# Routing an expert layer by a list of tokens: one-hot matmuls and gathers in place of a scatter of rows

## The chip, the cores and the metric

The kernel runs on one core of a Trainium2 chip. Its engines are TensorE (PE, with its weight loads as PEld), VectorE (DVE), ScalarE (ACT), GpSimd (POOL) and SyncE (SP). The metric is the time of one execution on the device in microseconds, lower is better.

## The reference

A decoder block over 32 sequences of 128 tokens with 128 features, 4096 tokens in all. Each of three layers is followed by a residual add and a layer norm.

```python
x = _layernorm(x + attn(x, Wq, Wk, Wv, Wo, betas))     # 16 heads, segments of 64
x = _layernorm(x + xattn(x, ctx, ctx, Wq, Wk, Wv))     # retention with decay
x = _layernorm(x + ffn(x, Wg, bg, W1, b1, W2, b2))

# ffn: top-1 routing over 8 experts, hidden size 512
gate_scores = softmax(x @ Wg + bg)
top1_idx = argmax(gate_scores)
top1_mask = one_hot(top1_idx, 8)
top1_weight = sum(gate_scores * top1_mask)
h = silu(einsum('btd,edh->bteh', x, W1) + b1)
o = einsum('bteh,ehd->bted', h, W2) + b2
y = sum(o * top1_mask[..., None], axis=2) * top1_weight
```

## The kernel before

The kernel is five phases, one after the other: `attention_phase`, `retention_phase`, `gate_phase`, `expert_phase` and `finish_phase`. Each opens a block in which every engine has a program of its own; engines wait for each other by semaphores, and a phase begins when all engines have ended the one before. Sequences lie as tiles of 128 tokens (partitions) by 128 features; groups are of four tiles (`G`).

`retention_phase` works over eight groups. PE transposes the context and x1, projects, scores, and multiplies; VectorE first computes the norm (`norm_dve`, lines 137 to 156) and then stages x1 (line 1007) and scales. GpSimd, before its own loop, fills a tile `padding` with zeros and a row number (lines 880 and 882). SyncE loads the expert weights after the last context tile (line 872) and then writes `padding` to the DRAM tensor `sorted_x` (line 874).

`gate_phase` norms again, keeps x2 in `x2_row` with the token's row in a 129th column, and computes logits. VectorE then runs one chain from line 1181 to 1247: softmax, the one-hot row of the best expert (`hot`), a prefix over the 32 batches in five doubling steps, and the row in expert order of each token (`place`); PE ranks tokens inside a batch by two matmuls (lines 1109 and 1110). The experts' tokens are padded to whole tiles of 128, at most `NT` = 39 tiles. GpSimd scatters the 32 tiles of `x2_row` into `sorted_x`, one indirect transfer each (line 1142).

`expert_phase` has 39 steps. SyncE loads `xs` from `sorted_x` in four pieces. For each tile ACT stages x and the biases (lines 1367 and 1374), PE transposes (1327), VectorE stages the expert's W1 (1410) and the transposed x (1414), PE computes the hidden layer (1343), ACT applies Silu (1392), PE multiplies by W2 (1353), and VectorE adds the bias (1433). GpSimd casts the row numbers and scatters the tile into `y_rows` (lines 1309 to 1314). `finish_phase` reads `y_rows` back, adds, norms and stores.

The order of work inside an engine is the order of its program; nothing is reordered. The steps of a loop are written once and unrolled in pairs by `run_steps`.

Of the kernel before, what the change touches and what calls it, by code (L numbers as in the profile page):

```python
# [6 lines left out]
F32 = mybir.dt.float32  # L7
F32R = mybir.dt.float32r
U32 = mybir.dt.uint32
# [23 lines left out]
NT = B + E - 1  # L33


def shape_constants():
# [25 lines left out]
    below = (tok[:, None] < tok[None, :]).astype(np.float32)  # L62
    ones = np.ones((P, P), np.float32)
    upto = row(np.arange(E)[None, :] <= np.arange(E)[:, None])
    tile_at = row(np.arange(NT))
    full = row(P * np.arange(B))
    token_row = tok[:, None] + P * np.arange(B)[None, :]
    spare_row = P * B + tok[:, None] + P * np.arange(NT)[None, :]
    cols = [ident, z_sum] + tabs + [decay, iota, below, ones, upto, tile_at, full, token_row, spare_row]
# [5 lines left out]
for _n, _w in (("ident", P), ("z_sum", SEG * H), ("qcos", P), ("qsin", P), ("kcos", P), ("ksin", P),  # L75
               ("decay", P), ("iota", E), ("below", P), ("ones", P), ("upto", E * E),
               ("tile_at", NT), ("full", B), ("token_row", B), ("spare_row", NT)):
    CONST_AT[_n] = (_at, _at + _w)
    _at += _w
# [732 lines left out]
def retention_phase(nc, const, r_all, stats, ctx_in, Wq, Wk, Wv, preload, sorted_x):  # L812
# [3 lines left out]
    with ExitStack() as ctx:  # L816
# [23 lines left out]
        padding = sb("padding", [P, NT, D + 1])  # L840
# [4 lines left out]
        padded, preloaded = sem("padded"), sem("preloaded")  # L845
# [12 lines left out]
        def _(sp):  # L858
# [172 lines left out]
def gate_phase(nc, const, r_all, x2_row, stats, top, tile_expert, biases, Wg, bg, b1, sorted_x):  # L1031
# [6 lines left out]
    with ExitStack() as ctx:  # L1038
# [14 lines left out]
        total, inv, index = (sb(n, [P, B]) for n in ("total", "inv", "index"))  # L1053
        b1_rows = sb("b1_rows", [E * FT, P])
        count, upto_batch = sb("count", [P, B, E]), [sb(f"upto_batch{i}", [P, B, E]) for i in range(2)]
        is_full, tiles, by_expert = sb("is_full", [P, E, B]), sb("tiles", [P, E]), sb("by_expert", [P, E, E])
        tile_end, tile_start = sb("tile_end", [P, E]), sb("tile_start", [P, E])
        after, expert_f = sb("after", [P, NT, E - 1]), sb("expert_f", [P, NT])
        row_of, place_f = sb("row_of", [P, B, E]), sb("place_f", [P, B])
        place = ctx.enter_context(nc.sbuf_tensor("place", [P, B], U32))  # L1060
        b1_bank = ctx.enter_context(nc.psum_tensor("b1_bank", [P, BANK], F32))
        rank_bank = ctx.enter_context(nc.psum_tensor("rank_bank", [P, 2, B, E], F32))
# [8 lines left out]
        hot_ready, ranked, placed, scattered = sem("hot_ready"), sem("ranked"), sem("placed"), sem("scattered")  # L1071
        block = ctx.enter_context(nc.Block())

        @block.sync
        def _(sp):
            sp.dma_start(wg[:, :], Wg).then_inc(w_loaded, 16)
            sp.dma_start(bg_rep[:, :], bg.rearrange("(o e) -> o e", o=1).to_broadcast([P, E])).then_inc(w_loaded, 16)
            sp.dma_start(b1_rows[:, :], b1.rearrange("e (f p) -> (e f) p", p=P)).then_inc(w_loaded, 16)

        @block.tensor  # L1080
        def _(pe):
# [26 lines left out]
            flat = hot[:, :, :].rearrange("p b e -> p (b e)")  # L1108
            pe.matmul(rank_bank[:, 0, :, :].rearrange("p b e -> p (b e)"), cst("below"), flat, start=True, stop=True)
            pe.matmul(rank_bank[:, 1, :, :].rearrange("p b e -> p (b e)"), cst("ones"), flat, start=True, stop=True).then_inc(ranked, 1)  # L1110

        @block.scalar
        def _(act):
# [11 lines left out]
            act.wait_ge(done, 2)  # L1125
            act.activation(ex[:, :, :], logits[:, :, :], ACT.Exp).then_inc(exp_done, 1)

        @block.gpsimd
        def _(pool):
# [8 lines left out]
            pool.tensor_copy(x2_row[:, :, D:].rearrange("p b o -> p (b o)"), cst("token_row")).then_inc(x2_kept, 1)  # L1138
            pool.wait_ge(x2_kept, NG + 1)
            pool.wait_ge(placed, 1)  # L1140
            for b in range(B):
                pool.indirect_dma_start(sorted_x, bass.IndirectOffsetOnAxis(ap=place[:, b:b + 1], axis=0),
                                        x2_row[:, b, :], None).then_inc(scattered, 16)
            pool.wait_ge(scattered, 16 * B)

        @block.vector
        def _(dve):
# [35 lines left out]
            dve.tensor_tensor(logits[:, :, :], logits[:, :, :], bc(top), ALU.subtract).then_inc(done, 1)  # L1183
            dve.wait_ge(exp_done, 1)
            dve.tensor_reduce(total[:, :], ex[:, :, :], X, ALU.add).then_inc(done, 1)
            dve.wait_ge(done, 3)
            dve.reciprocal(inv[:, :], total[:, :]).then_inc(done, 1)
            dve.wait_ge(done, 4)
            dve.tensor_tensor(ex[:, :, :], ex[:, :, :], bc(inv), ALU.mult).then_inc(done, 1)
            dve.wait_ge(done, 5)  # L1190
            dve.tensor_reduce(top[:, :], ex[:, :, :], X, ALU.max).then_inc(done, 1)
            dve.wait_ge(done, 6)

# [374 lines left out]
```

## Time and profile before

| | |
|---|---|
| median of 3 runs | 901.7 us (901.68 to 901.89) |
| profiled execution | 903.15 us |
| its span, first to last instruction | 901.3 us |
| mean granted TensorE clock | 0.899 |
| PE busy | 712.1 us (79%) |
| DVE busy | 605.1 us (67%) |
| ACT busy | 528.7 us (59%) |
| POOL busy | 513.4 us (57%) |

The durations further on come from the one profiled execution; its time outside the span is 1.85 us. A busy share is a mean over all phases. The attention phase, up to about 601 us, is most of the span and keeps every engine busy; the phases behind it do not. In rows, a number in square brackets is the idle time of the engine just before the instruction, with what ended it; PEq, POOLq and SPq are the sequencers of these engines. PEclk is the granted clock as a part of 2.4 GHz.

### The profile page before, as it was taken

The numbers are of one execution on the slowest core, as the hardware profiler recorded it, in microseconds if no ns is written. First come the engines' busy times: TensorE is split into PE (matmuls) and PEld (weight loads), VectorE is DVE, ScalarE is ACT, GpSimd is POOL, SyncE is SP. The second block draws the span as 40 slices with busy tenths as digits, with TensorE's granted clock in tenths as the row PEclk, the third lists the DMA queues.
The fourth block names the chain that finished last, engine by engine and source line by source line (L and its number), as shares of the span: only waits on it lengthen the run. The fifth ranks groups of instructions, "written<-read, shape, count | busy, mean of one in ns | idle before, by whom it ended". The sixth has DMA issues, their size and how long they took to land. (4 is left out here: it accounts for less than half of the span.)

```text
span 901.3 us, 26782 instructions
## 1 busy us (share of the span) xinstructions
PE 712.1 (79%) x9501; PEld 597.7 (66%) x9502; DVE 605.1 (67%) x1217; ACT 528.7 (59%) x1119; POOL 513.4 (57%) x524
## 2 busy tenths in 40 slices
PE   4789999999999999999999999748994600599920
PEld 3577788788778778778778877645664500598920
DVE  4378788788788788878878878745885510244438
ACT  3677787788788778778778878321221100477720
POOL 2167667757757756766765775633431167266742
PEclk8799999999999999999999999967996555699975
DMA  7567767767667677676776776611093011400033
GB/s 239 117 179 200 187 170 205 176 163 215 171 161 216 172 172 199 178 183 177 197 180 170 209 171 162 160 32 36 25 284 51 0 39 53 124 32 29 32 108 93
DMA packets 122154, 127.72 MB, mean 142 GB/s; under 512 B 7424, under 2 KB 101920, under 8 KB 118032
## 3 DMA queue, kind: packets, MB, share of 16 engines
q1 hardware_dynamic: 119584, 122.17, 52.8%
q0 software_dynamic: 2544, 5.21, 1.7%
q8 instruction: 15, 0.25, 0.1%
q14 instruction: 11, 0.09, 0.0%
HBM read 67.42 MB, written 43.16 MB: 123 GB/s over the span
## 5 line engine op out<-in xcount | busy, mean ns | idle before, releaser
L328 POOL TENSOR_TENSOR lhs<-pos_qv,ungate 64x1024 f32<-64x1024 f32 x64 | 151.7, 2370 | 161.9 <-PE mix L495 151.2
L614 ACT ACTIVATE psT<-bank 128x512 f32<-128x512 f32 x128 | 72.6, 594 | 92.5 <-PE bank L484 92.5
L766 DVE TENSOR_TENSOR lhs<-mix,zg_all 64x512 f32<-64x512 f32 x128 | 88.2, 689 | 5.8 <-PE mix L467 1.9
L353 POOL TENSOR_TENSOR e_qk<-e_qk 128x512 f32<-128x512 f32 (+2 forms) x96 | 78.6, 819 | 20.1 <-DVE e_qk L707 15.1
L484 PE MATMUL bank<-const,ps 128*128 128x128 f32 x512 | 70.0, 280 | 21.7 <-POOL ps L343 21.5
L598 ACT ACTIVATE e_qk<-e_qk 128x512 f32<-128x512 f32 x128 | 82.3, 643 | 0.0
L721 DVE TENSOR_REDUCE s_max<-bank 128x8 f32<-128x512 f32 x64 | 44.2, 691 | 48.7 <-PE bank L453 47.8
L467 PEld LDWEIGHTS mix<-pos_qv 64*64 64x64 f32 (+1 forms) x2048 | 65.6, 137 | 13.7 <-issue 11.2
L484 PEld LDWEIGHTS bank<-const,ps 128*128 128x128 f32 x512 | 55.2, 142 | 27.9 <-issue 15.7
L574 ACT ACTIVATE qk_tok<-bank 128x512 f32<-128x512 f32 x128 | 73.2, 601 | 0.0
L603 ACT ACTIVATE qkT<-bank 128x512 f32<-128x512 f32 x128 | 71.2, 610 | 1.8 <-PE bank L430 1.0
L467 PE MATMUL mix<-pos_qv 64*64 64x64 f32 (+1 forms) x2048 | 72.2, 225 | 0.0
L495 PE MATMUL mix<-psT,lhs 128*64 128x64 f32 x2048 | 69.7, 229 | 3.0 <-DVE lhs L766 2.2
L495 PEld LDWEIGHTS mix<-psT,lhs 128*64 128x64 f32 x2048 | 65.3, 143 | 8.6 <-issue 8.6
L389 PE MATMUL bank<-w_k,x_cur 128*128 128x512 f32 x192 | 63.6, 442 | 7.5 <-ACT psT L614 7.5
L430 PE MATMUL bank<-const,qk_tok 128*128 128x128 f32 x512 | 67.2, 273 | 2.7 <-DVE e_qk L707 2.1
L1410 DVE COPY w_cur<-w 128x512 f32 x39 | 16.8, 431 | 77.3 <-issue 48.6
L512 PE MATMUL bank<-w_o,attT 128*128 128x128 f32 x512 | 65.2, 282 | 4.0 <-DVE attT L700 4.0
L512 PEld LDWEIGHTS bank<-w_o,attT 128*128 128x128 f32 x512 | 61.0, 195 | 10.7 <-ACT qkT L603 7.1
L430 PEld LDWEIGHTS bank<-const,qk_tok 128*128 128x128 f32 x512 | 59.4, 140 | 12.8 <-DVE e_qk L707 2.5
L343 POOL TENSOR_TENSOR ps<-s_exp,row_rec 128x512 f32<-128x512 f32 x64 | 65.4, 1042 | 0.0
L336 POOL TENSOR_TENSOR ps<-pos_qv,sq_rec 128x1024 f32<-128x1024 f32 x32 | 60.9, 1902 | 5.9 <-POOL lhs L328 4.8
(212 smaller groups left out, 1694.5 us busy)
## 6 DMA issues: line engine op xcount, KB each, us to landing
scratch_qv<-qv_out SPq DMA_DIRECT2D x32, 1024.0 KB, 5.7
pos_qv<-scratch_qv SPq DMA_DIRECT2D x64, 512.0 KB, 6.6
swapT<-qkT SPq DMA_DIRECT2D x64, 256.0 KB, 4.0
zg_all<-scratch_z SPq DMA_DIRECT2D x64, 256.0 KB, 3.8
sorted_x<-padding SPq DMA_DIRECT2D x1, 2515.5 KB, 18.5
r_all<-in_x_dram SPq DMA_DIRECT2D x4, 512.0 KB, 7.0
cx<-in_ctx_dram SPq DMA_DIRECT2D x8, 256.0 KB, 2.7
w<-in_L_ffn_W_dram SPq DMA_DIRECT2D x1, 2048.0 KB, 9.7
```

Source lines behind the costliest of these rows:

```text
L328: pool.tensor_tensor(lhs[0:L, 1 - n, :, :], pos_qv[s, :, DK:], ungate[s, :, :], ALU.mult).then_inc(vg_ready, 1)
L353: pool.tensor_tensor(dst, e_qk[:, 0:c, DK:], e_qk[:, c:2 * c, DK:], ALU.add).then_inc(k_summed, 1)
L430: last = pe.transpose(qk_bank[f][:, i * P:(i + 1) * P], qk_tok[:, 4 * f + i, :], cst("ident"))
L467: last = pe.matmul(mix[odd * DK:(odd + 1) * DK, h // 8, at:at + DK], pos_qv[0:k, h, 0:DK], pos_qv[0:k, h, DK:], start=True, stop=True)
L484: last = pe.transpose(turn_bank[f % 2][:, i * P:(i + 1) * P], ps[:, 4 * f + i, :], cst("ident"))
L495: last = pe.matmul(mix[odd * DK:(odd + 1) * DK, n, at:at + L], lhs[:, 1 - n, h, :], psT[:, h, n * L:(n + 1) * L], start=True, stop=True)
L512: last = pe.matmul(score_bank[1][:, 0:D], attT[:, c, :], w_o[:, c, :], start=(c == 0), stop=(c == C // 2 - 1))
L574: act.activation(qk_tok[:, 8 * hh:8 * hh + 8, slot * DK:(slot + 1) * DK], half_bank(bank, hh), ACT.Copy).then_inc(evac, 1)
L598: act.activation(e, e, ACT.Exp, scale=-1.0).then_inc(grown, 1)
L603: act.activation(qkT[:, :, 4 * f:4 * f + 4], qk_bank[f][:, :].rearrange("p (c s) -> p s c", c=4), ACT.Copy).then_inc(qkT_evac, 1)
L614: act.activation(psT[:, 4 * f:4 * f + 4, :], turn_bank[f % 2][:, :].rearrange("p (h s) -> p h s", h=4), ACT.Copy).then_inc(psT_evac, 1)
L766: dve.tensor_tensor(dst, mix[odd * DK:(odd + 1) * DK, g, :].rearrange("p (i n k) -> p i n k", n=SEG, i=4), zg_all[odd * DK:(odd + 1) * DK, ...
```

## The change

The padding and its write to `sorted_x` are dropped. `gate_phase` takes the best expert from the logits, not from the softmax; it computes the prefix over batches by one scan, and rounds by integer masks. x2 is no longer scattered: SyncE writes it in token order, with the weight `top` in the 129th column, to the DRAM tensor `x2_rows`. Which token lies in which row of the expert order is found on chip: VectorE compares each token's tile number and its row in the tile with all possible ones (`at_tile`, `in_row`), GpSimd and ACT scale the first by the batch and the token (`in_tile`), and 32 matmuls of `in_row` by `in_tile` add up a list, from which come `token_of` and `row_to`. The weight `top` is now the reciprocal of the sum of exponentials.

In `expert_phase` GpSimd gathers each of the 39 tiles by `token_of`, twelve ahead of the work and then in groups of four, and scatters each y by `row_to`. A memset of `mark` raises the semaphore `gathered`, on which ACT waits for every tile. `y` has 39 buffers in place of two. The reciprocal is taken after the comparisons; `tile_expert` follows it.

```diff
 NT = B + E - 1
+AHEAD = 12
...
-        padding = sb("padding", [P, NT, D + 1])
...
-            sp.wait_ge(padded, 2)
-            sp.dma_start(sorted_x.rearrange("(t p) d -> p t d", p=P), padding[:, :, :]).then_inc(preloaded, 16)
-            sp.wait_ge(preloaded, 16 * (len(preload) + 1))
+            sp.wait_ge(preloaded, 16 * len(preload))
-            pool.memset(padding[:, :, :], 0.0).then_inc(padded, 1)
-            pool.wait_ge(padded, 1)
-            pool.tensor_copy(padding[:, :, D:].rearrange("p t o -> p (t o)"), cst("spare_row")).then_inc(padded, 1)
...
+            sp.wait_ge(x2_kept, NG)
+            sp.wait_ge(top_kept, 1)
+            sp.dma_start(x2_rows.rearrange("(b p) d -> p b d", p=P), x2_row[:, :, :]).then_inc(x2_stored, 16)
+            sp.wait_ge(x2_stored, 16)
...
+            pe.matmul(rank_bank[:, 1, :, :], cst("ones"), by_expert(hot[:, :, :]), start=True, stop=True)
+            pe.matmul(rank_bank[:, 0, :, :], cst("not_below"), by_expert(hot[:, :, :]), start=True, stop=True).then_inc(ranked, 1)
+            for b in range(B):
+                if b % G == 0:
+                    pe.wait_ge(in_row_ready, b // G + 1)
+                if b % (B // 2) == 0:
+                    pe.wait_ge(in_tile_ready, b // (B // 2) + 1)
+                    pe.wait_ge(token_ready, b // (B // 2) + 1)
+                last = pe.matmul(list_bank[:, 0:2 * NT], in_row[:, b, :], in_tile[:, b, :, :].rearrange("p o t -> p (o t)"), start=(b == 0), stop=(b == B - 1))
+            last.then_inc(listed, 1)
...
+            act.wait_ge(shifted, 1)
+            for i in range(2):
+                half_b = slice(i * B // 2, (i + 1) * B // 2)
+                act.wait_ge(placed, i + 1)
+                act.activation(in_tile[:, half_b, 1, :], at_tile[:, half_b, :], ACT.Copy, scale=cst("token")).then_inc(token_ready, 1)
+            act.wait_ge(top_ready, 1)
+            act.activation(x2_row[:, :, D:].rearrange("p b o -> p (b o)"), top[:, :], ACT.Copy).then_inc(top_kept, 1)
...
-            pool.wait_ge(placed, 1)
-            for b in range(B):
-                pool.indirect_dma_start(sorted_x, bass.IndirectOffsetOnAxis(ap=place[:, b:b + 1], axis=0),
-                                        x2_row[:, b, :], None).then_inc(scattered, 16)
-            pool.wait_ge(scattered, 16 * B)
+            for i in range(2):
+                half_b = slice(i * B // 2, (i + 1) * B // 2)
+                dims = [P, B // 2, NT]
+                pool.wait_ge(placed, i + 1)
+                pool.tensor_tensor(in_tile[:, half_b, 0, :], at_tile[:, half_b, :],
...
+            dve.tensor_tensor(hot[:, :, :], logits[:, :, :], bc(top), ALU.is_equal).then_inc(done, 1)
+            dve.scalar_tensor_tensor(hot[:, :, :], hot[:, :, :], -float(E), iota, ALU.mult, ALU.add).then_inc(done, 1)
+            dve.tensor_reduce(index[:, :], hot[:, :, :], X, ALU.min).then_inc(done, 1)
+            dve.scalar_tensor_tensor(hot[:, :, :], iota, -float(E), bc(index), ALU.add, ALU.is_equal).then_inc(hot_ready, 1)
+            dve.tensor_tensor(logits[:, :, :], logits[:, :, :], bc(top), ALU.subtract).then_inc(shifted, 1)
+            dve.wait_ge(ranked, 1)
+            dve.tensor_tensor_scan(upto_batch[:, :, :].rearrange("p e b -> p (e b)"), cst("first"),
+                                   rank_bank[:, 1, :, :].rearrange("p e b -> p (e b)"), 0.0, ALU.mult, ALU.add).then_inc(done, 1)
+            last_of = upto_batch[:, :, B - 1:].rearrange("p e o -> p (e o)")
+            dve.tensor_scalar(padded[:, :], last_of, P - 1.0, None, ALU.add).then_inc(done, 1)
+            dve.tensor_tensor(row_of[:, :, :], upto_batch[:, :, :], rank_bank[:, 0, :, :], ALU.add).then_inc(done, 1)
+            dve.tensor_scalar(tiles[:, :], padded[:, :], WHOLE, None, ALU.bitwise_and).then_inc(done, 1)
+            dve.tensor_tensor_scan(tile_end[:, :], cst("ones")[:, 0:E], tiles[:, :], 0.0, ALU.mult, ALU.add).then_inc(done, 1)
+            dve.tensor_tensor(tile_start[:, :], tile_end[:, :], tiles[:, :], ALU.subtract).then_inc(done, 1)
+            dve.tensor_tensor(row_of[:, :, :], row_of[:, :, :], tile_start[:, :].unsqueeze(2).to_broadcast([P, E, B]),
+                              ALU.add).then_inc(done, 1)
+            dve.tensor_tensor(row_of[:, :, :], row_of[:, :, :], by_expert(hot[:, :, :]), ALU.mult).then_inc(done, 1)
+            dve.tensor_reduce(place_f[:, :], row_of[:, :, :].rearrange("p e b -> p b e"), X, ALU.add).then_inc(done, 1)
+            dve.tensor_copy(place[:, :], place_f[:, :]).then_inc(done, 1)
+            dve.tensor_scalar(tile_u[:, :], place[:, :], WHOLE, None, ALU.bitwise_and).then_inc(done, 1)
+            dve.tensor_scalar(row_u[:, :], place[:, :], P - 1, None, ALU.bitwise_and).then_inc(done, 1)
+            for g in range(NG):
+                if g % (NG // 2) == 0:
+                    s = slice(G * g, G * g + B // 2)
+                    dims = [P, B // 2, NT]
+                    dve.tensor_tensor(at_tile[:, s, :], cst("tile_at").unsqueeze(1).to_broadcast(dims),
+                                      tile_u[:, s].unsqueeze(2).to_broadcast(dims), ALU.is_equal).then_inc(placed, 1)
+                s = slice(G * g, G * g + G)
+                dve.tensor_tensor(in_row[:, s, :], cst("lane").unsqueeze(1).to_broadcast([P, G, P]),
+                                  row_u[:, s].unsqueeze(2).to_broadcast([P, G, P]), ALU.is_equal).then_inc(in_row_ready, 1)
+            dve.reciprocal(top[:, :], total[:, :]).then_inc(top_ready, 1)
+            dve.wait_ge(listed, 1)
+            dve.tensor_copy(token_at[:, :], list_bank[:, NT:2 * NT])
+            dve.tensor_scalar(empty[:, :], list_bank[:, 0:NT], 0.0, None, ALU.is_equal).then_inc(done, 1)
+            dve.scalar_tensor_tensor(token_at[:, :], list_bank[:, 0:NT], float(P), token_at[:, :], ALU.mult, ALU.add).then_inc(done, 1)
+            dve.scalar_tensor_tensor(empty[:, :], cst("spare_row"), float(P), empty[:, :], ALU.add, ALU.mult).then_inc(done, 1)
+            dve.tensor_scalar(token_of[:, :], token_at[:, :], -float(P), 0.0, ALU.add, ALU.max)
+            dve.scalar_tensor_tensor(row_to[:, :], token_at[:, :], -float(P), empty[:, :], ALU.add, ALU.add)
...
+            def gather(t):
+                pool.indirect_dma_start(xs[:, t, :], None, x2_rows,
+                                        bass.IndirectOffsetOnAxis(ap=token_of[:, t:t + 1], axis=0)).then_inc(x_loaded[t % (AHEAD + G)], 16)
+
+            def publish(a, z):
+                for t in range(a, z):
+                    pool.wait_ge(x_loaded[t % (AHEAD + G)], 16 * (t // (AHEAD + G) + 1))
+                pool.memset(mark[:, a:z], 0.0).then_inc(gathered, z - a)
+
+            def scatter(t):
+                pool.wait_ge(y_added, t + 1)
+                pool.indirect_dma_start(y_rows, bass.IndirectOffsetOnAxis(ap=row_to[:, t:t + 1], axis=0),
+                                        y[:, t, :], None).then_inc(stored, 16)
+
+            for t in range(AHEAD):
+                gather(t)
+                if t > 1:
+                    publish(t - 2, t - 1)
+            publish(AHEAD - 2, AHEAD)
+            for t in range(0, NT, G):
+                ahead = t + AHEAD
+                for i in range(ahead, min(ahead + G, NT)):
+                    gather(i)
+                for i in range(t, min(t + G, NT)):
+                    scatter(i)
+                if ahead < NT:
+                    publish(ahead, min(ahead + G, NT))
+                if ahead < NT <= ahead + G:
+                    pool.memset(xs[:, NT:, :], 0.0).then_inc(gathered, 1)
+            pool.wait_ge(stored, 16 * NT)
...
+                act.wait_ge(gathered, t + 1)
...
-                    if not is_step(t, 1, 2):
-                        dve.wait_ge(stored[q], 16 * (half if p == 1 else half - 1))
-                    dve.tensor_tensor(y[q][:, :], y_bank[q][:, 0:D], b_cur[q][:, FT:],
+                    dve.tensor_tensor(y[:, bass.ds(u, 1), :].rearrange("p o d -> p (o d)"), y_bank[q][:, 0:D], b_cur[q][:, FT:],
```

## Rows read from the trace of the kernel before

**Rows 1.** Timeline, start of retention: start us, us, engine, line, operation, tiles.

```profile
601.82 4.29 POOL L880 MEMSET padding<- 128x5031 f32 x1 [12.47 <-POOLq L176]
...
601.86 0.22 DVE L137 TENSOR_TENSOR r_mean<-stats 128x32 f32<-128x32 f32 x1 [0.31 <-PEq L176]
...
602.36 3.78 DVE L141 TENSOR_SCALAR r_mean<-r_mean 128x32 f32<-128x32 f32 x1
...
609.60 1.12 PE L918 MATMUL r_x1t<-const,x 128*128 128x128 f32 x4 [2.27 <-DVE x L1007]
```

**Rows 2.** Waits of SyncE: who waited for what, us in total, times, longest.

```profile
SPq L816 <- DMA sorted_x<-padding: 16.9, 1, 16.9
```

**Rows 3.** Timeline of the gate phase, VectorE and PE.

```profile
684.90 0.21 DVE L137 TENSOR_TENSOR g_mean<-stats 128x32 f32<-128x32 f32 x1 [4.30 <-PEq L816]
...
710.17 0.19 DVE L1156 TENSOR_TENSOR logits<-g_logit,bg_rep 128x32 f32<-128x32 f32 x1 [1.51 <-PE g_logit L1102]
...
715.21 0.42 DVE L1202 TENSOR_TENSOR hot<-index,const 128x256 f32<-128x256 f32 x1
...
716.70 1.06 PE L1110 MATMUL rank_bank<-hot,const 128*128 128x256 f32 x2
...
724.96 0.18 DVE L1247 CAST place<-place_f 128x32 uint32<-128x32 f32 x1
```

**Rows 4.** Timeline of GpSimd from the first scatter to the last.

```profile
726.02 1.08 POOL L1142 DMA_INDIRECT sorted_x<-x_row,place  x1 [19.91 <-DVE place L1247]
...
771.02 0.20 POOL L1295 MEMSET xs<- 128x129 f32 x1 [4.48 <-POOLq L1038]
...
863.80 0.99 POOL L1314 DMA_INDIRECT y_rows<-y,row  x1 [0.15 <-issue]
```

**Rows 5.** DMA issues: count, KB each, median us to landing.

```profile
sorted_x<-padding SPq DMA_DIRECT2D x1, 2515.5 KB, 18.5
...
out_dram<-o SPq DMA_DIRECT2D x8, 256.0 KB, 2.2
...
sorted_x<-x_row,place POOLq DMA_INDIRECT x32, 2.3
```

**Rows 6.** Timeline of the expert phase, PE, one pair of tiles apart.

```profile
842.15 1.13 PE L1343 MATMUL h_bank_a<-e_xT,w_cur 128*128 128x128 f32 x8 [0.24 <-ACT hT L1392]
...
846.39 1.13 PE L1343 MATMUL h_bank_a<-e_xT,w_cur 128*128 128x128 f32 x8 [0.21 <-ACT hT L1392]
```

**Rows 7.** Timeline: operations near in size to the new ones.

```profile
626.61 2.06 DVE L1007 TENSOR_SCALAR x<-r_all,r_mean,r_rstd 128x128 f32 x4
...
674.53 1.26 POOL L896 TENSOR_TENSOR kh<-k_cos,k_sin 128x512 f32<-128x512 f32 x1 [0.45 <-DVE k_sin L1024]
...
677.06 0.69 DVE L1016 TENSOR_TENSOR sc<-r_score,const 128x512 f32<-128x512 f32 x1
...
701.80 1.72 PE L1102 MATMUL g_logit<-wg,x2T 128*128 128x8 f32 x8
...
704.04 1.11 DVE L1167 TENSOR_SCALAR x<-r_all,g_mean,g_rstd 128x128 f32 x4
```

**Rows 8.** Windows: us, busy us (count) of each engine, PEclk, DMA share, GB/s.

```profile
590.00:591.00 1.00, 1.00 (x7) 0.93 (x7) 0.00 (x0) 0.63 (x2) 0.00 (x0) 0.61 0.00 0
...
672.00:674.00 2.00, 2.00 (x9) 1.04 (x8) 1.62 (x3) 0.00 (x0) 1.19 (x1) 1.00 1.24 178
...
780.00:782.00 2.00, 2.00 (x14) 2.00 (x14) 0.58 (x2) 0.42 (x2) 0.00 (x0) 0.66 0.76 180
```

**Rows 9.** Groups by line, 705 to 866 us: busy us, mean ns, idle before.

```profile
L1314 POOL DMA_INDIRECT y_rows<-y,row x39 | 42.2, 1083 | 13.4 <-DMA y_rows<-y,row 7.8 <-issue 5.6
...
L1142 POOL DMA_INDIRECT sorted_x<-x_row,place x32 | 31.1, 971 | 29.4 <-DVE place L1247 19.9 <-issue 9.4
```

**Rows 10.** Line 1314 alone: duration ns min/median/max, first and last start.

```profile
L1314 POOL DMA_INDIRECT y_rows<-y,row x39: 989/993/1252, 782.7 to 863.8; - x39
```

**Rows 11.** Timeline of the end of attention, PE.

```profile
588.49 1.07 PE L484 MATMUL bank<-const,ps 128*128 128x128 f32 x8 [2.37 <-POOL ps L343]
```

More of the change, by code:

```diff
@@ L61, in shape_constants @@
     iota = row(np.arange(E))
-    below = (tok[:, None] < tok[None, :]).astype(np.float32)
+    not_below = (tok[:, None] < tok[None, :]).astype(np.float32) - 1.0
     ones = np.ones((P, P), np.float32)
[L64 to L67, printed above, removed]
+    tile_at = row(P * np.arange(NT))
+    first = row(np.tile(np.arange(B) > 0, E))
+    batch = row(np.arange(B) + 1)
+    token = tok[:, None].astype(np.float32)
+    lane = row(np.arange(P))
     spare_row = P * B + tok[:, None] + P * np.arange(NT)[None, :]
-    cols = [ident, z_sum] + tabs + [decay, iota, below, ones, upto, tile_at, full, token_row, spare_row]
+    cols = [ident, z_sum] + tabs + [decay, iota, not_below, ones, tile_at, first, batch, token, spare_row, lane]
     return np.ascontiguousarray(np.concatenate(cols, axis=1).astype(np.float32))
@@ L75 @@
 for _n, _w in (("ident", P), ("z_sum", SEG * H), ("qcos", P), ("qsin", P), ("kcos", P), ("ksin", P),
-               ("decay", P), ("iota", E), ("below", P), ("ones", P), ("upto", E * E),
-               ("tile_at", NT), ("full", B), ("token_row", B), ("spare_row", NT)):
+               ("decay", P), ("iota", E), ("not_below", P), ("ones", P),
+               ("tile_at", NT), ("first", E * B), ("batch", B), ("token", 1), ("spare_row", NT), ("lane", P)):
     CONST_AT[_n] = (_at, _at + _w)
@@ L1028, in _, with gate_phase @@
             residual(NG - 1)
-def gate_phase(nc, const, r_all, x2_row, stats, top, tile_expert, biases, Wg, bg, b1, sorted_x):
+def gate_phase(nc, const, r_all, x2_row, stats, top, tile_expert, token_of, row_to, biases, Wg, bg, b1, x2_rows):
     with ExitStack() as ctx:
@@ L1194, in _ @@
-            dve.tensor_tensor(hot[:, :, :], ex[:, :, :], bc(top), ALU.is_equal).then_inc(done, 1)
-            dve.wait_ge(done, 7)
-            dve.tensor_scalar(hot[:, :, :], hot[:, :, :], -float(E), float(E), ALU.mult, ALU.add).then_inc(done, 1)
-            dve.wait_ge(done, 8)
-            dve.tensor_tensor(hot[:, :, :], hot[:, :, :], iota, ALU.add).then_inc(done, 1)
-            dve.wait_ge(done, 9)
-            dve.tensor_reduce(index[:, :], hot[:, :, :], X, ALU.min).then_inc(done, 1)
-            dve.wait_ge(done, 10)
@@ L1215, in _ @@
-            upto, spare = upto_batch[cur], upto_batch[1 - cur]
-            dve.wait_ge(done, n)
-            dve.tensor_tensor(is_full[:, :, :], upto[:, B - 1, :].unsqueeze(2).to_broadcast([P, E, B]),
-                              cst("full").unsqueeze(1).to_broadcast([P, E, B]), ALU.is_gt).then_inc(done, 1)
-            dve.tensor_tensor(spare[:, :, :], upto[:, :, :], count[:, :, :], ALU.subtract).then_inc(done, 1)
-            dve.wait_ge(done, n + 1)
-            dve.tensor_reduce(tiles[:, :], is_full[:, :, :], X, ALU.add).then_inc(done, 1)
@@ L1239, in _ @@
-            dve.wait_ge(done, n + 8)
+            dve.wait_ge(done, 17)
+            dve.reciprocal(top[:, :], total[:, :]).then_inc(top_ready, 1)
+            dve.wait_ge(done, 18)
             dve.tensor_reduce(expert_f[:, :], after[:, :, :], X, ALU.add).then_inc(done, 1)
-            dve.wait_ge(done, n + 9)
-            dve.tensor_tensor(row_of[:, :, :], row_of[:, :, :], hot[:, :, :], ALU.mult).then_inc(done, 1)
-            dve.wait_ge(done, n + 11)
-            dve.tensor_reduce(place_f[:, :], row_of[:, :, :], X, ALU.add).then_inc(done, 1)
+            dve.wait_ge(done, 19)
@@ L1253, in expert_phase @@
+def expert_phase(nc, const, w1, w2, biases, tile_expert, token_of, row_to, x2_rows, y_rows):
     with ExitStack() as ctx:
```

149 lines of the change are left out of this document (48 added, 101 removed).

## The prediction

> **What bounds the kernel now.** I read the trace stage by stage, because the edits touch only boundaries and three late stages, and each stage starts when every engine has arrived and every transfer it waits for has landed. The timeline at the start of retention shows VectorE held up: the `tensor_scalar` of the mean, 0.2 us elsewhere, is shown with 3.78 and ends with GpSimd's 4.29 us memset of `padding`, and the chain behind it is late by as much. PE's first x1 transpose follows at 609.60, 2.27 us after its context transposes were done at 607.33 [rows 1]. The waits of SyncE show what ends retention: 16.9 us of waiting for the write of `padding` to `sorted_x` [rows 2]. VectorE began the gate phase at 684.90 after 4.30 us of idle time, so its retention work ended at 680.60 [rows 3].
>
> In the gate phase one chain on VectorE sets the pace: the last bias add ends at 710.36, `hot` at 715.63, PE's ranking at 717.76, `place` at 725.14 [rows 3]. Then GpSimd alone works: 32 scatters, the first at 726.02; the expert phase starts at 771.02 after 4.48 of idle time, so the last was issued at 765.57 and ended at 766.54, 1.276 us from start to start [rows 4]. A scatter lands 2.3 us after its issue, at 767.9, so the boundary costs 3.1 us more when GpSimd has sent indirect transfers; between attention and retention it costs 0.31 [rows 1, 4, 5]. In the expert phase PE takes two tiles in 4.24 us [rows 6]; GpSimd's 39 scatters of y fit under it. The last one is issued at 863.80, 92.8 us after the phase began [rows 4].
>
> **The change part by part.** Numbers are positions in the old trace; savings add up.
>
> *Retention, start.* Without the memset the stalled operations take their usual 0.2. VectorE's chain then comes some 3.5 us earlier, but PE is held by its context transposes, which wait for a load and end at 607.33. The x1 transposes move from 609.60 to 607.35: **−2.25** (bounds 0 and −3.5). PE and VectorE are busy from there on, so I let it survive.
>
> *Retention, end.* Without the padding write the other preloads are older (the bias load lands before). The boundary then follows VectorE's end at 680.60 by 0.3, as in [rows 1]: 684.90 becomes 680.9, **−3.95** (bounds 0 and −4.0).
>
> *Gate, argmax.* Ten operations and an exponential between 710.36 and 715.63 become five of 0.42 with 0.04 between: 2.3 us in place of 5.27, −2.97. The ranking matmuls, 2.13 us, are the same with another order of columns; I take the same price.
>
> *Gate, places.* After the ranking, 7.38 us become: a scan of 256, which no row shows (0.42 as an add of this size, up to twice its 0.27 us of data, 0.69; I take 0.6), then an add 0.42, three small ones 0.6, add, multiply and reduction 1.35, cast and two masks 0.6: 3.7.
>
> *Gate, one-hot tables.* Two comparisons of 624 elements and eight of 512. The row for 512 is 0.69 [rows 7]; with the overlap of neighbours I take 0.61 to 0.62 each and 0.75 for the larger: 6.5. Behind them reduction, comparison and reciprocal: 1.2; ACT copies `top` into the row: 0.3. GpSimd multiplies 624 elements twice beside this, about 1.3 to 1.5 each by its row of 512 at 1.26. Such pairs hold each other up: four `tensor_scalar` of x take 2.06 beside GpSimd's add and 1.11 alone, 0.95 more [rows 7]. I take 1.1 for each half, 2.2 together (bounds 0 and 3.0).
>
> The Trainium skill (SBUF — State Buffer, Who interferes with whom) says that a VectorE operation with two SBUF inputs and a GpSimd operation that reads SBUF block each other for a whole instruction; these comparisons are such. The rows agree, the memset included, which held back only operations that can use the second port. By it the two halves cost up to 3.0 and the sum would be 0.8 higher than by the rows.
>
> So `top_kept` comes 3.7+6.5+1.2+0.3+2.2 = 13.9 after the ranking, which ends at 714.79 in old positions: 728.7.
>
> *Gate, the new store.* SyncE now writes x2 with `top` to `x2_rows`, 2064 KB in rows of 516 bytes, and only after `top_kept`. The nearest row is the padding write with the same row length: alone it moved 178 GB/s [rows 8], and 2.11 MB at that are 11.8 us; with issue and landing I take 12.5. Bounds: 8 us (an output store of 256 KB, with rows of 512 bytes, lands in 2.2 [rows 5]; eight of them overlapped some 1 us apart) and 18.5 (the whole padding write, part of it beside another load). It lands at 741.2, and the boundary is 0.5 (0.31 by [rows 1], and SyncE's wait): 741.7. This store, not the list, ends the phase: PE's 32 list matmuls start near 721.5, cold at 0.43 each (by the logit matmuls, also with 128-column weights and at 1.2 GHz, 1.72 for four [rows 7]) end by 735.3, and six small operations follow to 736.7, 4 us ahead. The 32 scatters, 40 us, are gone from here. 771.02 to 741.7: **−29.3**.
>
> *Expert phase.* GpSimd now issues 39 gathers and 39 scatters. No row shows a gather; the nearest is the scatter of the same rows. Nothing of it lies ahead of the phase, so it costs queue time: 0.9 before the first (as 725.14 to 726.02), 77 steps of 1.276 = 98.3, some 19 `mark` and pad memsets at 0.1 more than the issue gap = 2.0, and 1.3 for the landing of the twelfth gather: 102.5 to the last scatter's issue. In the old loop a scatter took 1.083 on average against 0.971 in the quiet stretch [rows 9]: 66 of them lie beside VectorE's copies, between 0.02 and 0.112 dearer, 1.3 to 7.4; I take 4.4. That is 106.9 against 92.8: **+14.1** (bounds +10 and +24, the latter with 1.25 busy for all 66, the longest seen). GpSimd is thus the bound: eight transfers a group are some 10.8 us, and PE needs 8.5 for four tiles. ACT waits for `gathered` at tile t+2 before it does the Silu of t+1, so once PE has used up the twelve tiles of lead (around tile 14) it stands some 2.3 us in every group. The waits of scatters on `y_added` are met: tile 38 is done about 12 us after the last publish, some 2 us ahead of its turn.
>
> *The rest.* The dropped waits on `stored`, the row casts and the carrier lay under PE or on GpSimd's old loop, and are in the above. The constants grow by 289 columns, loaded at the start; the first user is the k sum, behind the projections of the first batch, and if that cover were gone it would cost under 1 us: nothing.
>
> **Sum.** 901.3 −2.25 −3.95 −29.3 +14.1 = 879.9. This execution took 903.15, 1.85 around its span; the median is 1.45 below that. So the median should be 879.9+0.4, about **880 us**.
>
> **The rivals.**
>
> 1. *Gathers are dear, and it ends slower.* Everything gained is lost when each of the 39 gathers costs 21.4/39 = 0.55 us more than a scatter, a step of 1.83. If it took two scatters' time (2.55), 39 × 1.276 = 49.8 more: 930. For it: no row shows a gather, and nothing hides it. Against: the 39 scatters of the loop lie between 0.989 and 1.252 [rows 10]. Chance 0.05.
>
> 2. *The port.* If every tile's copy of w1 (0.43) keeps GpSimd out in full, some 34 tiles cost 14.6 in place of 4.4: 890. For it: the scatters of 1.25 begin under that copy. Against: others beside it take 0.99. The Trainium skill (SBUF — State Buffer, SBUF: two separate sides) has this as a rule: descriptors can't be written while VectorE copies in its two-port mode. Chance 0.15.
>
> 3. *PE's clock falls in the new gaps.* In the old trace a gap of 2.37 us before 588.49 [rows 11] was followed by a granted clock of 0.61 from 590 to 591, and in the expert phase, begun at 771, PE was back at 2.4 GHz only at 781 (0.66 from 780 to 782) [rows 8]. Such a spell costs 3.6 us of PE time per group; a group needs 12.1, above GpSimd's 10.8, and the last tile comes some 8 us late: 888. Chance 0.10.
>
> 4. *Retention gives nothing*, because a load or another transfer takes over both ends: 880+6.2 = 886. Chance 0.08.
>
> 5. The forecast, 873 to 887: 0.57. The remaining 0.05 is a faster store (8 us) with cheap contention, 870 to 873, or faster.
>
> Range 870 to 893: it leaves out rival 1 and a tail of rivals 2 and 3. Within 0.2%, which is about what this measurement can tell from no change, lies 0.01; slower by more 0.05; faster 0.94.
>
> **What would show it.** Retention starts PE's x1 near 607.4 and the gate phase follows VectorE's end by 0.3; `x2_rows` is issued about 42 us after the gate phase began, lands 12 to 13 us later, and the next phase follows at once; GpSimd's indirect transfers stand 1.27 to 1.4 us apart and fill the expert phase of about 107 us; ACT waits for `mark` from tile 14 on. The forecast is wrong if gathers are longer than 1.1 us busy, if the store takes over 18 us, or if the list is later than the store.

## The result, and the profile after

The changed kernel takes 922.7 us (median of 4 runs, 920.29 to 928.19) against 901.7 (899.56 to 901.89): a ratio of 1.025, 95% interval 1.020 to 1.030. It is slower by 2.5%, where 880 us and faster were forecast. The profiled execution took 920.29 us, with a span of 918.5.

First the boundaries and the gate phase, in the timeline of the kernel after:

```profile
596.98 0.29 DVE L697 BATCH_NORM_STATS2 stats<-r_all 128x6 f32<-128x128 f32 x1
597.60 0.21 DVE L140 TENSOR_TENSOR r_mean<-stats 128x32 f32<-128x32 f32 x1 [0.32 <-PEq L179]
...
602.73 1.06 PE L914 MATMUL r_x1t<-const,x 128*128 128x128 f32 x4
...
672.97 0.21 DVE L140 TENSOR_TENSOR g_mean<-stats 128x32 f32<-128x32 f32 x1 [0.31 <-PEq L819]
...
701.83 1.10 PE L1119 MATMUL rank_bank<-hot,const 128*128 128x256 f32 x2
...
702.98 0.69 DVE L1216 TENSOR_TENSOR_SCAN upto_batch<-const,rank_bank 128x256 f32<-128x256 f32 x1 [1.96 <-PE rank_bank L1119]
...
707.68 3.52 DVE L1248 TENSOR_TENSOR in_row<-const,row_u 128x512 fp32r<-128x512 f32 x4
...
716.69 0.39 SPq L1087 DMA_DIRECT2D x_rows<-x_row  x1
...
718.04 0.18 DVE L1267 TENSOR_SCALAR token_of<-token_at 128x39 uint32<-128x39 f32 x1
...
731.33 1.09 POOL L1306 DMA_INDIRECT xs<-x_rows,token_of  x1 [17.71 <-SPq L1274]
...
876.76 0.97 POOL L1316 DMA_INDIRECT y_rows<-y,row_to  x1 [0.50 <-DVE y L1438]
...
885.85 5.11 SPq L1474 DMA_DIRECT2D y_tok<-y_rows  x7
...
888.78 1.14 DVE L1509 SCALAR_TENSOR_TENSOR r_all<-y_tok,top,x_row 128x128 f32<-128x128 f32 x4 [12.30 <-DMA y_tok<-y_rows]
```

Up to the expert phase nearly all went as forecast. PE's x1 transposes follow the end of attention (597.27) by 5.5 us in place of 8.1 [rows 1]; the gate phase follows VectorE's last work by 0.31 in place of 4.30 [rows 3]; the store is issued 13.8 us after the ranking, and the expert phase begins at 731.33 in place of 771.02 [rows 4]. The one surprise there is luck: this execution's attention phase, which no edit touches, ended 4.3 us sooner. In the 14 traces of this case it ended anywhere between 597.0 and 601.9.

From there on the 39.7 us gained so far are given back, and 17 more. The last scatter of y is issued 145.4 us after the phase began, against 92.8 before [rows 4] and 106.9 forecast. The page of the kernel after shows that GpSimd isn't the bound:

```profile
L1316 POOL DMA_INDIRECT y_rows<-y,row_to x39 | 38.1, 978 | 56.2 <-DVE y L1438 53.3
```

The line is busy us, mean ns, idle before it. A scatter takes 0.98 us, a gather 0.97, yet the scatters waited 53.3 us for VectorE's y. And the waits by engine hold something that the kernel before never had, a releaser "remote". It means that the semaphore which ended the wait was raised over 1.5 us after the work that the profile shows to raise it; shorter delays are not counted. Of the list of waits:

```profile
POOL y_rows L1316 <- DVE y L1438: 53.3, 30, 3.3
...
DVE e_xT L1424 <- remote: 27.7, 7, 5.6
...
ACT hT L1406 <- remote: 27.2, 12, 3.6
...
DVE y L1438 <- remote: 9.3, 2, 5.5
```

The numbers are us in total, times, longest. The three remote waits are together 64.2 us. One such place, in the timeline of the kernel after:

```profile
792.96 0.99 POOL L1306 DMA_INDIRECT xs<-x_rows,token_of  x1 [0.19 <-issue]
...
793.07 1.13 PE L1358 MATMUL h_bank_a<-e_xT,w_cur 128*128 128x128 f32 x8 [0.16 <-ACT hT L1406]
...
794.04 0.27 PE L1342 MATMUL e_turn<-const,e_x 128*128 128x128 f32 x1
...
794.14 1.06 PE L1368 MATMUL y_bank<-w,hT 128*128 x8
794.26 0.96 POOL L1306 DMA_INDIRECT xs<-x_rows,token_of  x1 [0.30 <-issue]
...
796.18 0.62 ACT L1406 ACTIVATE hT<-h_bank_a,b_cur 128x128 f32<-128x128 f32 x2 [2.40 <-remote]
...
798.03 0.99 POOL L1316 DMA_INDIRECT y_rows<-y,row_to  x1 [0.30 <-issue]
800.32 0.62 ACT L1406 ACTIVATE hT<-h_bank_a,b_cur 128x128 f32<-128x128 f32 x2 [3.52 <-remote]
800.36 0.29 DVE L1424 COPY e_xT<-e_turn 128x128 f32<-128x128 f32 x1 [5.64 <-remote]
800.58 0.29 DVE L1438 TENSOR_TENSOR y<-y_bank,b_cur 128x128 f32 x1
```

PE's hidden layer is recorded as done at 794.2, its transpose at 794.31, its y at 795.2. VectorE copies the transpose, for which it waits for PE alone, at 800.36; ACT does the second half of the Silu at 800.32. Between 793 and 799 GpSimd issues five transfers, some 1.27 us apart, and the engines go on 2.3 us after the last issue, about the time in which such a transfer lands [rows 5]. PE's clock falls in these gaps: busy us (count) of PE, PEld, VectorE, ACT and GpSimd, then the clock, after:

```profile
760.00:780.00 20.00, 16.32 (x102) 15.65 (x101) 5.22 (x16) 9.44 (x34) 11.79 (x14) 0.78 0.15 36
780.00:800.00 20.00, 10.44 (x68) 10.11 (x68) 4.03 (x13) 7.44 (x26) 10.12 (x12) 0.82 0.14 36
800.00:820.00 20.00, 13.43 (x80) 13.21 (x81) 5.28 (x16) 9.26 (x33) 8.89 (x10) 0.76 0.11 30
```

### The profile page after: what moved, and what is told of

The parts are those of the page before. It is cut to its first block and busy times, and to the rows that moved or that the text cites. A ratio compares the mean times of both kernels' runs of the same rounds, so it can differ in the third digit from the quotient of the medians.

```text
span 918.5 us, 26677 instructions
## 1 busy us (share of the span) xinstructions
PE 733.8 (80%) x9533; PEld 619.8 (67%) x9534; DVE 607.7 (66%) x1219; ACT 532.2 (58%) x1122; POOL 501.6 (55%) x470
## 5 line engine op out<-in xcount | busy, mean ns | idle before, releaser
L356 POOL TENSOR_TENSOR e_qk<-e_qk 128x512 f32<-128x512 f32 (+2 forms) x96 | 78.6, 818 | 18.8 <-DVE e_qk L710 13.8
L724 DVE TENSOR_REDUCE s_max<-bank 128x8 f32<-128x512 f32 x64 | 44.2, 691 | 50.6 <-PE bank L456 49.7
L470 PEld LDWEIGHTS mix<-pos_qv 64*64 64x64 f32 (+1 forms) x2048 | 64.8, 136 | 13.4 <-issue 11.1
L487 PEld LDWEIGHTS bank<-const,ps 128*128 128x128 f32 x512 | 55.5, 142 | 26.4 <-issue 14.1
L498 PE MATMUL mix<-psT,lhs 128*64 128x64 f32 x2048 | 67.5, 225 | 2.8 <-DVE lhs L769 2.0
L1316 POOL DMA_INDIRECT y_rows<-y,row_to x39 | 38.1, 978 | 56.2 <-DVE y L1438 53.3
L498 PEld LDWEIGHTS mix<-psT,lhs 128*64 128x64 f32 x2048 | 63.1, 139 | 8.2 <-issue 8.2
L433 PEld LDWEIGHTS bank<-const,qk_tok 128*128 128x128 f32 x512 | 60.0, 141 | 11.7 <-ACT qk_tok L577 1.6
L392 PE MATMUL bank<-w_v,x_cur 128*128 128x512 f32 x192 | 60.1, 423 | 5.6 <-DVE w_v L681 3.4
## 6 DMA issues: line engine op xcount, KB each, us to landing
x_rows<-x_row SPq DMA_DIRECT2D x1, 2064.0 KB, 13.5
```

Of the source, the lines that this page charges most:

```text
L356: pool.tensor_tensor(dst, e_qk[:, 0:c, DK:], e_qk[:, c:2 * c, DK:], ALU.add).then_inc(k_summed, 1)
L392: last = pe.matmul(bank[hh][:, :], x_cur[p][:, x_at, :], w[:, w_at, hh * BANK:(hh + 1) * BANK], start=(i == 0), stop=(i == 2))
L433: last = pe.transpose(qk_bank[f][:, i * P:(i + 1) * P], qk_tok[:, 4 * f + i, :], cst("ident"))
L470: last = pe.matmul(mix[odd * DK:(odd + 1) * DK, h // 8, at:at + DK], pos_qv[0:k, h, 0:DK], pos_qv[0:k, h, DK:], start=True, stop=True)
L487: last = pe.transpose(turn_bank[f % 2][:, i * P:(i + 1) * P], ps[:, 4 * f + i, :], cst("ident"))
L498: last = pe.matmul(mix[odd * DK:(odd + 1) * DK, n, at:at + L], lhs[:, 1 - n, h, :], psT[:, h, n * L:(n + 1) * L], start=True, stop=True)
```

## The experiments

Theory A: a row of indirect transfers makes what PE hands to ACT and VectorE arrive late. The rivals put it on the gathers as such (B), on the loops (C), on the engines' loads of the expert number (D), or on bytes. Runs without a ratio were made once.

**1. No gathers** (`no_gathers`, called kernel 1 below). Up to experiment 7, edits of GpSimd's program are in `expert_phase`.

```diff
+            for i in range(3):
+                a, z = CUTS[i], CUTS[i + 1]
+                sp.dma_start(xs[:, a:z, :], rows[:, a:z, :]).then_inc(x_loaded[i], 16)
+            sp.dma_start(xs[:, 24:NT, :], rows[:, 17:32, :]).then_inc(x_loaded[3], 16)
...
+            for i in range(4):
+                pool.wait_ge(x_loaded[i], 16)
+                pool.memset(mark[:, CUTS[i]:CUTS[i + 1]], 0.0).then_inc(gathered, CUTS[i + 1] - CUTS[i])
+            pool.memset(xs[:, NT:, :], 0.0).then_inc(gathered, 1)
+            for t in range(NT):
+                scatter(t)
```

> The changed kernel without gathers: SyncE loads xs from x2_rows in four plain pieces, so the tiles hold other tokens than the list says, and seven tiles are loaded twice. List, scatters and the rest are as they were. If the gathers are what delays the other engines (A and B), the expert phase is back at 92 to 95 us, no wait of ACT or VectorE is put down to a remote release, and the kernel takes 866 to 872 us. If something else in the new loop is slow (39 buffers of y, waits of scatters on y_added without the extra add before them), the phase stays above 110 us and the kernel above 885.

Measured: 866.65 us, ratio to the kernel before 0.963 (0.958 to 0.969); no remote wait; the same stretches as above show PE at full clock:

```profile
760.00:780.00 20.00, 19.33 (x160) 18.20 (x159) 9.13 (x29) 15.30 (x56) 8.92 (x10) 1.00 0.09 30
780.00:800.00 20.00, 19.15 (x158) 18.00 (x157) 8.82 (x29) 15.14 (x57) 8.90 (x10) 1.00 0.09 30
```

The last scatter is issued 92.4 us after the phase began. That is 53.0 us less than with the 39 gathers and 0.4 less than in the kernel before, so nothing else in the new loop costs any.

**2. Another order** (`one_by_one`): `gather(t + AHEAD)`, `scatter(t)` and a publish in turn.

> The changed kernel with its 39 gathers in other places of GpSimd's queue: after the first twelve, one gather and one scatter in turn, each gather published one tile later, in place of four gathers and four scatters. Theory A, signals of PE are held back while two or more indirect transfers are in flight: GpSimd still issues two a tile, some 1.27 us apart with 2.3 us to landing, so two are nearly always in flight; the stalls get shorter (under 2 us each) and more frequent, and the kernel takes 900 to 920 us. Theory B, only a row of four or more gathers does harm: the stalls vanish, the loop is bound by GpSimd at 2.6 us a tile, and it takes 882 to 890 us. If neither the order nor the burst matters: 920 to 925.

909.8 us, ratio 1.010 (1.005 to 1.015), remote waits 33.8. The time is in A's range, and far from 882 to 890, but the waits are not the short ones that A expected: the longest is 6.2 us. Spreading the same transfers halves the remote waits and takes 12.9 of the 56.1 us over kernel 1 away. It doesn't end the harm, since rows form again: from 812.07 on four transfers start some 1.28 us apart, and then GpSimd waits 1.7 us for y. It waits 36.9 us for y in all, so GpSimd isn't the bound here either.

**3. All gathers first** (`all_first`).

> The changed kernel with all 39 gathers in a row before the first scatter. Theory A: the gathers last 50 us without a pause, the other engines crawl in them (at most 12 tiles done by then), and the scatters follow at PE's pace, 2.15 us a tile: 50 + 27 x 2.15 = 108 us or more for the phase, and long waits on remote releases all within the first 50 us. If the gathers held nobody up, the tiles would be computed in some 87 us, and 50 + 39 x 1.27 = 100 us would be the phase, with no remote waits: 878 us in all.

911.7 us; 49.7 us of remote waits, one of 17.1. The gathers took 53 us, and in them VectorE added the y of one tile only (at 756.48, the next at 786.1), where A allowed up to twelve. The other 38 followed at about PE's pace, so the last scatter came 137 us into the phase. The timeline:

```profile
743.37 0.27 PE L1335 MATMUL e_turn<-const,e_x 128*128 128x128 f32 x1
...
743.48 1.06 PE L1361 MATMUL y_bank<-w,hT 128*128 x8
...
756.19 0.29 DVE L1431 TENSOR_TENSOR y<-y_bank,b_cur 128x128 f32<-128x128 f32 x1 [13.89 <-remote]
756.60 0.31 ACT L1382 ACTIVATE b_cur<-biases 128x132 f32 x1 [15.08 <-DVE y L1431]
...
766.13 0.62 ACT L1399 ACTIVATE hT<-h_bank_a,b_cur 128x128 f32<-128x128 f32 x2 [9.21 <-issue]
...
774.40 0.62 ACT L1399 ACTIVATE hT<-h_bank_a,b_cur 128x128 f32<-128x128 f32 x2 [7.65 <-remote]
774.44 0.29 DVE L1417 COPY e_xT<-e_turn 128x128 f32<-128x128 f32 x1 [17.07 <-remote]
```

PE's transpose, done at 743.64, is taken up at 774.44, 31 us later, with gathers in a row nearly all the while. VectorE's y, ended at 756.48 amid them, reaches ACT at 756.60. So it is not the waits of ACT or VectorE that fail, but what comes from PE. The trace also holds the times at which semaphores were raised, and they say the same: the transpose's is recorded at 774.41, 30.8 us after the transpose's recorded end, that of VectorE's y at 756.49, 0.01 after it.

**4. One gather in flight** (`one_in_flight`): `publish(i, i + 1)` right behind every `gather(i)`.

> The changed kernel with each gather published, so its landing waited for, before the next transfer is issued; groups of four as before. A gather then costs GpSimd some 2.7 us, a group 4 x 2.7 + 4 x 1.3 = 16 us, and the kernel is bound by GpSimd at about 920 us whatever the theory. What tells the theories apart is the waits: with A (two or more in flight) the remote waits of ACT and VectorE fall from 64 us to under 10; if any gather in flight holds PE's signals back, they stay above 30 us.

946.5 us, where about 920 was expected: a gather with its landing takes GpSimd 2.9 us, the first scatter comes 48 us into the phase, and GpSimd sets the pace. The remote waits fall to 13.0, above A's "under 10" and far below the 30 of the other case. Rows of scatters are left in this kernel, and there the waits stand: 1.9 us behind three scatters at 834.51 to 837.29, the other 11.1 in the row of 15 with which the phase ends.

**5. Rows of scatters alone, of 4, 3 and 2** (`scatter_groups`, `scatter_threes`, `scatter_pairs`). The edit against kernel 1, here with `G` for the row's length of 4 (3 and 2 in the others):

```diff
-            for t in range(NT):
-                scatter(t)
+            for t in range(0, NT, G):
+                pool.wait_ge(y_added, min(t + G, NT))
+                for i in range(t, min(t + G, NT)):
+                    scatter(i)
```

> The kernel without gathers (866.65 us as no_gathers, again with other tokens in xs than the list says), its 39 scatters of y issued in groups of four, once the fourth tile of the group is added, in place of one after each tile. Theory A, any two or more indirect transfers in flight hold back PE's signals: each group of four, some 5 us long and 8.5 us apart, delays the engines by 1 to 4 us, remote waits of 15 to 40 us appear, and it takes 880 to 905 us. Rival B, only gathers (writes into SBUF) do harm: no remote waits and 866 to 872 us.

> The kernel without gathers (other tokens in xs than the list says), its scatters of y issued two in a row after every second tile. One at a time it took 866.65 us, four in a row 896.18 with 45 us of remote waits. If the harm begins with the second transfer in flight (A as stated), pairs cost a good part of that: 10 to 30 us of remote waits, 872 to 890 us. If three or more in a row are needed, no remote waits and 866 to 870 us.

> The kernel without gathers (other tokens in xs than the list says), its scatters of y issued three in a row after every third tile. Pairs took 869.03 us with no remote wait, fours 896.18 with 45 us of them. If the harm begins with the third transfer in a row, threes show remote waits, 15 to 40 us, and 878 to 893 us; if it needs the fourth, none and 867 to 872 us.

| scatters in a row | us | remote waits, us |
|---|---|---|
| 1 | 866.65 | 0 |
| 2 | 869.03 | 0 |
| 3 | 881.24 | 17.2 |
| 4 | 896.18 | 45.1 |

Waits of the kernel with fours:

```profile
DVE e_xT L1426 <- remote: 26.1, 9, 3.3
...
ACT hT L1408 <- remote: 19.0, 11, 2.3
```

The same 39 transfers of the same bytes, only grouped, cost 29.5 us, with remote waits over A's 15 to 40. Grouping has a plain price too, since the last three scatters wait for the last y; it is small: from the phase's start to the last y it took 92.1 us in kernel 1, 106.7 with threes and 120.6 with fours, and only 2.5 more came behind it. The 2.4 us of the pairs lie within the spread of kernel 1 (864.47 to 872.29). Gathers aren't needed for it, so rival B falls. A as first stated, a good part of the harm from the second one on, falls too: in the pairs' trace PE's semaphores are raised up to 0.65 us late, which costs nothing that can be told.

**6. Few bytes** (`narrow_groups`): fours again, but of `y[:, i, 0:8]` into another tensor; the whole rows follow behind the loop.

> The kernel without gathers (other tokens in xs than the list says); in its loop GpSimd scatters only 8 columns of each tile of y, into another tensor, in groups of four; the 39 scatters of whole rows follow in a row behind the loop, some 50 us that have nothing beside them. If it is the number of row descriptors written in a row that holds PE's signals back, the loop is as slow as with whole rows: some 45 us of remote waits, and 896 + 49 = 945 us. If it is the bytes that they move (32 in place of 512 to a row), the loop takes its undisturbed time: no remote waits and 866.65 + 49 = 915 us.

945.8 us and 39.7 us of remote waits, as by the number of transfers and their rows (945 and some 45). A sixteenth of the bytes leaves nearly all of the harm. No run tells the number of transfers from that of their rows, 128 in each.

**7. The loops and the loads** (`unrolled`, `fixed_expert`): `run_steps` written out without a loop; `expert_of` gives 0.

> The changed kernel with the 39 steps of the expert phase written out for PE, ACT and VectorE, no loops: every wait is on a constant, no register is computed for it and no instruction is fetched again at a branch. Rival C, the engines stand because their loops' register work or instruction fetch is held up by the indirect transfers: the remote waits vanish and the time falls to 880 to 890 us. Theory A: the remote waits stay at 40 to 70 us and the time between 905 and 925.

> The changed kernel with expert 0 for every tile: PE, ACT and VectorE no longer load the tile's expert from tile_expert before each step, so the result is that of expert 0 alone; all transfers, copies and matmuls have the same sizes. Rival D, it is these loads (three a tile, each some 0.3 us by an engine's sequencer) that the rows of indirect transfers hold up: the remote waits vanish and it takes 880 to 890 us. If it is what PE hands over to ACT and VectorE that comes late, whatever the sequencers load: 40 to 70 us of remote waits and 905 to 925 us.

911.1 us with 40.7 us of remote waits, and 904.1 with 38.0. Neither is the cause: the remote waits don't vanish, and in the changed kernel's trace none of the 117 loads takes over 0.6 us. But both runs have fewer of them than the changed kernel's 64.2 and are 11.7 and 18.6 us faster, and without the loads time and waits are both just under A's range. Each was run once; why they have less, and how much of the gain is the plain price of a loop or of the loads, is open.

**8. The store** (`early_store`): `x2_rows` and `xs` 128 wide, stored in four pieces after every second `x2_kept`.

> The changed kernel with x2_rows 128 columns wide (the weight column is not read by the expert phase) and stored in four pieces as GpSimd finishes the copies of x2, in place of one store after top_kept. If the one late store is what ends the gate phase, the expert phase starts with the list, some 11 us earlier (718.9 in place of 730.7 in the same positions), and the kernel takes 909 to 912 us. If the store was covered, 920 to 923.

910.6 us. The expert phase began 46.5 us after the gate phase in place of 58.5 (ACT's first work in each): 12.0 us for holding the store back for a column that the expert phase doesn't read.

**9. A version without gathers** (`scatter_and_list`).

```diff
+            sp.dma_start(sorted_x.rearrange("(t p) d -> p t d", p=P),
+                         cst("ident").unsqueeze(1).to_broadcast([P, NT, D])).then_inc(filled, 16)
...
-                pool.wait_ge(placed, i + 1)
-                pool.tensor_tensor(in_tile[:, half_b, 0, :], at_tile[:, half_b, :],
...
+            for b in range(B):
+                pool.indirect_dma_start(sorted_x, bass.IndirectOffsetOnAxis(ap=place[:, b:b + 1], axis=0),
+                                        x2_row[:, b, 0:D], None).then_inc(scattered, 16)
...
+                    dve.tensor_tensor(in_tile[:, s, 0, :], at_tile[:, s, :],
...
```

> A version that avoids gathers: x2 is scattered into sorted_x in the gate phase as in the kernel before, 32 transfers in a row with no computation that waits for PE beside most of them; the list by one-hot matmuls is kept, computed beside the scatters, and gives only the rows of y (VectorE multiplies by the batch in place of GpSimd). sorted_x is filled with finite numbers from a constant tile by one write at the start of the gate phase. The expert phase is that of no_gathers with real rows. Expected from rows: places known 34 us after the gate phase starts, 31 x 1.27 + 1 us of scatters, 3.1 to the next phase: the expert phase starts some 19 us later than in no_gathers, 866.65 + 19.5 = 886 us (880 to 892). If VectorE's comparisons hold up the scatters by 0.3 each, up to 5 us more. Slower than 895 would say that the list's waits for PE are held back by the scatters beyond their end.

889.65 us, ratio to the kernel before 0.987 (0.984 to 0.991): 1.3% less than before, and less than the changed kernel. The expert phase begins 23.8 us later than in kernel 1, where 19.5 was expected. GpSimd in the timeline:

```profile
707.80 1.20 POOL L1165 DMA_INDIRECT sorted_x<-x_row,place  x1 [13.55 <-DVE row_u L1240]
...
748.87 0.96 POOL L1165 DMA_INDIRECT sorted_x<-x_row,place  x1 [0.30 <-issue]
756.88 0.10 POOL L1333 MEMSET mark<- 128x3 f32 x1 [7.04 <-DMA xs<-sorted_x]
...
847.74 0.97 POOL L1328 DMA_INDIRECT y_rows<-y,row_to  x1 [0.55 <-DVE y L1441]
```

It keeps the long row of transfers where almost nothing waits for PE, and in the expert phase it mostly has one transfer a tile, and no remote wait. One handover from PE does stand in the long row, and it was on time: VectorE reads the list 0.05 us after PE's last matmul for it, with seven transfers issued by then and PE at 1.2 GHz.

**Which handovers are late.** The table takes VectorE's copy of PE's transpose in the expert phases of 12 kernels (the changed one and all of these but the last, 40 copies each): its start, minus the later of PE's end and VectorE's own last end. "In a row" counts issues less than 1.75 us apart, the last of them under 2.3 us before PE's end. The clock is by the transpose's own length (0.27 us at 2.4 GHz, 0.42 at 1.2).

| in a row | at 2.4 GHz: over 1 us late | at 1.2 GHz |
|---|---|---|
| 0 or 1 | 0 of 270 | 0 of 51 |
| 2 | 14 of 50 | 0 of 12 |
| 3 or more | 42 of 71 | 4 of 26 |

All 14 late ones of the line of 2 stand in rows that went on to three or more; in rows that stayed at two, none of 30 at 2.4 GHz was late. Of what VectorE hands to ACT (`b_cur` after y, 25 cases where y came last) all went on within 0.03 us, of what ACT hands to PE (`e_turn` after `e_x`, 41 cases) all within 0.05, 11 of the 66 beside three or more in a row.

The semaphores show it without a choice of cases. In the expert phases of all 14 traces, every recorded raising by ACT (2808) and by VectorE (1460) comes 0.01 us after the recorded end of its work, 293 of them beside three or more in a row. Of PE's 1978, 419 come over 0.1 us after it. (Some raisings are missing from the traces.)

## Why the prediction was wrong

| step | forecast | measured |
|---|---|---|
| attention (no edit) | 0 | −4.3 |
| retention, start and end | −2.25, −3.95 | −2.6, −4.0; −1.1 more between |
| gate phase | −29.3 | −27.8 |
| expert phase to the last scatter | +14.1 | +52.7 |
| boundary behind it, finish | 0 | +3.1, +1.1 |
| sum, on 901.3 | 879.9 | 918.5 |

**The step that failed** is "GpSimd is thus the bound", with "the waits of scatters on `y_added` are met". The forecast priced 78 transfers as time of GpSimd's queue, and that price was right: 0.97 us each, no dearer than a scatter, at 1.27 apart. But GpSimd, forecast to be busy without a pause, waited 53.3 us for VectorE's y. What the forecast left out, and so put at nothing without a reason, is that a row of transfers delays the other engines. Kernel 1 takes the gathers out and gets the 53 us back; the fours of experiment 5 cost 29.5 us without a gather. The ending that came, slower, was given 0.05, and for another mechanism: gathers are not dear (rival 1), and the harm is in their rows.

**Rival 2, the port.** The contention term of 4.4 us was close to nothing: all gathers lie between 0.947 and 1.131 us, and those beside VectorE's copies of w1 take 0.99 on average, the others 0.96. Nor does the port explain the stalls: ACT stands as long as VectorE does, and from 796.8 to 800.3 with VectorE idle throughout. The Trainium skill (SBUF — State Buffer, SBUF: two separate sides) says that transfers and engines cannot slow each other, but for the shared port of VectorE and GpSimd. The runs agree as far as bytes go, by `narrow_groups`; yet by that rule alone experiment 5 would show next to no difference, and it shows 29.5 us. The measurement decides: transfers did hold up the work of the engines, by way of what PE hands over.

**Rival 3, the clock,** came as a consequence: the granted clock was 0.76 to 0.82 in the stretches of 20 us between 740 and 840, and PE is busy 733.8 us, where kernel 1, which has the same matmuls, has 718.5. So some 15 us of PE time went to the lower clock. It is a part of the 52.7, not beside it.

**Right in mechanism, off in size.** The store landed 13.5 us after its issue (forecast 12.5). Of each four comparisons the one beside GpSimd's multiplication took 1.72 us and the others 0.68, so a half cost 1.0 more (forecast 1.1). The list's matmuls took 0.225 each at 1.2 GHz in place of 0.43: their operands are fp32r, and the trace has one record for each, where an fp32 logit matmul has two. The upper bound of the expert phase doesn't add up: 66 transfers of 1.25 us in place of 0.971 give 102.5 + 18.4 = 120.9, +28 and not +24; the measured +52.7 lies beyond either. The scan took 0.69 (forecast 0.6, bound 0.69). The Trainium skill (DVE: opcode table, instruction layouts, handler registers and perf-mode slots, Datapath and trigger behaviour) says that the scan runs at half throughput; the trace agrees, 0.69 against 0.41 for the add of the same 256 elements behind it. That `top_kept` and the store end the gate phase, the list 12 us ahead (forecast 4), was taken as given and not questioned; `early_store` shows that this cost 12.0 us for nothing.

What stays open: the trace shows that PE's matmuls are recorded on time and that its semaphores are raised late. PE's ends are modelled, so it can't tell whether its results are late as well. No run shows what in a transfer does the harm, whether GpSimd's issuing of it, its 128 rows, or the signals of its landing. Nor does any run show why PE at 2.4 GHz is hit so much harder than at 1.2, or the first transfer of a row not at all.

## What to carry to other kernels

An indirect transfer has two prices: its time in GpSimd's queue, and what a row of three or more does to engines that wait for PE. Keep rows of them for stretches in which nobody waits for PE, and elsewhere issue one or two and let them land. When a new resource is used beside a tight loop of three engines, its own price, however well known, bounds the time from below only; the forecast's range should have had the loop slowed, not just GpSimd's queue.

## What the runs showed of the hardware

- Indirect transfers in a row, some 1.27 us apart, delay what PE hands over by up to 31 us (`all_first`). Of scatters, 2 in a row cost nothing that can be told (2.4 us in 39 tiles), 3 in a row 14.6, 4 in a row 29.5 (one run each), and rows of 32 bytes do nearly as much as rows of 512 (39.7 and 45.1 us of remote waits).
- What ACT and VectorE hand over is not delayed: all 4268 recorded raisings of their semaphores in the expert phases come 0.01 us after their work.
- Behind the expert phase VectorE's first add follows the last scatter's issue by 8.8 to 9.0 us (the kernel before, kernel 1 and the others) where the phase had 39 indirect transfers and by 11.9 to 12.2 (the changed kernel and the others with 78). No edit explains these 3 us, and no run shows their cause.
